# A mixture-of-experts stage in a vision tower: the routing weights come to all partitions by a broadcast transfer instead of a selecting matmul

## The reference, cut to what matters

```python
topk_idx, topk_w = _gate(x, gate_w, gate_bias)      # 8 of 32 experts for each token, with weights
g = jnp.einsum('th,eih->eti', x, expert_gate)
u = jnp.einsum('th,eih->eti', x, expert_up)
outs = jnp.einsum('eti,ehi->eth', jax.nn.silu(g) * u, expert_down)
outs_t = jnp.transpose(outs, (1, 0, 2))
gathered = jnp.take_along_axis(outs_t, topk_idx[:, :, None], axis=1)
final = (gathered * topk_w[:, :, None]).sum(1)
shared = _mlp(residuals, shared_gate, shared_up, shared_down)
return final.reshape(orig_shape) + shared
```

## Time and profile before

| | |
|---|---|
| median of 3 runs | 427.67 us (426.64 to 428.51) |
| profiled execution, span from first to last instruction | 425.9 us |
| TensorE busy | 394.3 us, 93% |
| VectorE busy | 265.4 us, 62% |
| ScalarE busy | 187.7 us, 44% |
| GpSimd busy | 145.9 us, 34% |
| mean granted TensorE clock | 0.988 of full speed |

### The profile page before, as it was taken

How to read it: one execution, slowest core, us unless ns; L and a number is a source line. 1 busy time by engine, 2 the same in 40 slices (tenths; PEclk the granted TensorE clock), 3 DMA queues, 4 the chain that set the end, 5 groups by cost and what they waited for, 6 DMA issues and landing times.

```text
span 425.9 us, 8795 instructions
## 1 busy us (share of the span) xinstructions
PE 394.3 (93%) x3362; PEld 319.3 (75%) x3362; DVE 265.4 (62%) x529; ACT 187.7 (44%) x401; POOL 145.9 (34%) x119
## 2 busy tenths in 40 slices
PE   8998699898999799999999999999988999999684
PEld 6654478656786689999999999999986765567342
DVE  0368886688876875555555555555554648854776
ACT  0244832248242534444444444444435378734161
POOL 0145300363032153333333333333384246720102
PEclk9999999998999999999999999999999999999799
DMA  8930000200051022222222222232000000000001
GB/s 303 339 148 0 3 3 2 98 1 3 4 186 37 2 74 75 75 75 74 74 74 74 74 74 74 74 79 68 0 0 2 0 2 2 2 2 2 0 0 58
DMA packets 9547, 23.79 MB, mean 56 GB/s; under 512 B 1264, under 2 KB 3248, under 8 KB 9008
## 3 DMA queue, kind: packets, MB, share of 16 engines
q1 hardware_dynamic: 7632, 21.49, 15.8%
q10 hardware_dynamic: 1888, 1.93, 1.3%
HBM read 22.81 MB, written 0.61 MB: 55 GB/s over the span
## 4 chain that ended last, share of the span: by engine, by line
PE 71%; DVE 21%; issue 4%; ACT 4%; POOL 0%; DVEq 0%; ACTq 0%
PE psum L1073 70%; DVE xn L764 3%; DVE rc L838 3%; DVE nt L761 2%; DVE rn L817 1%; DVE nt L759 1%; DVE rn L816 1%; ACT region L716 1%; DVE region L839 1%; DVE xc L750 1%; DVE ra L807 1%; DVE km L1055 1%; ACT sq L532 1%; PE psum L1225 1%; DVE km L827 1%
## 5 line engine op out<-in xcount | busy, mean ns | idle before, releaser
L1073 PE MATMUL psum<-xh,split_all 128*128 128x296 f32 x544 | 122.1, 299 | 1.4 <-DVE rt L918 1.3
L431 POOL TENSOR_TENSOR split_all<-km,split_all 128x768 fp32r<-128x768 f32 x34 | 62.7, 1845 | 119.8 <-ACT split_all L645 119.8
L1073 PEld LDWEIGHTS psum<-xh,split_all 128*128 128x128 f32 x544 | 91.4, 188 | 1.9 <-DVE rt L918 1.9
L1073 PE MATMUL psum<-xl,split_all 128*128 128x296 f32 (+1 forms) x288 | 84.8, 299 | 0.0
L1073 PE MATMUL psum<-ah,split_all 128*128 128x296 f32 x272 | 73.5, 324 | 2.9 <-DVE al L981 2.4
L665 ACT ACTIVATE ah<-rt 128x296 fp32r<-128x296 f32 x68 | 30.7, 452 | 94.7 <-DVE rt L979 88.0
L1073 PEld LDWEIGHTS psum<-xl,split_all 128*128 128x128 f32 (+1 forms) x288 | 53.2, 187 | 3.2 <-issue 3.2
L976 DVE TENSOR_TENSOR rb<-ra,psum 128x296 f32<-128x296 f32 x64 | 29.6, 462 | 41.3 <-PE psum L1073 29.9
L981 DVE TENSOR_TENSOR al<-rt,ah 128x296 fp32r<-128x296 f32 x64 | 31.6, 495 | 33.2 <-ACT ah L665 33.2
L1073 PEld LDWEIGHTS psum<-ah,split_all 128*128 128x128 f32 x272 | 48.6, 192 | 4.1 <-DVE al L981 2.8
L1073 PE MATMUL psum<-al,split_all 128*128 128x296 f32 x136 | 40.6, 299 | 0.0
(11 more groups left out here) (181 smaller groups left out, 612.5 us busy)
## 6 DMA issues: line engine op xcount, KB each, us to landing
km<-in_experts SPq DMA_DIRECT2D x34, 384.0 KB, 3.0
w_sb<-in_w SPq DMA_DIRECT2D x2, 1024.0 KB, 11.8
region<-in_x SPq DMA_DIRECT2D x6, 296.0 KB, 5.5
region<-in_g_wo SPq DMA_DIRECT2D x1, 1024.0 KB, 4.8
region<-in_l_wo SPq DMA_DIRECT2D x1, 1024.0 KB, 4.8
region<-in_w_lin ACTq DMA_DIRECT2D x6, 128.0 KB, 6.7
qkv_sb<-in_qkv_w SPq DMA_DIRECT2D x1, 768.0 KB, 6.0
cst<-in_consts ACTq DMA_DIRECT2D x1, 504.5 KB, 6.8
```

What stands on the lines that cost most here:

```text
L431: nc.gpsimd.tensor_tensor(wl[i], ring[i], wh[i].bitcast(f32), ALU.subtract)\
L1073: return nc.tensor.matmul(out_, lhsT, rhs, start=start, stop=stop, skip_group_check=True)
```

## The change

The weights are no longer split into three bf16 parts. They are transposed in f32 by products with the identity, copied to `wrow` (now 32 rows x 640 columns, f32, in two copies), written to a DRAM tensor `weights`, and read back for each expert by one transfer that puts its row of 592 values on all 128 partitions of a slot of `wb`, a ring of four. VectorE's second product reads `wb` in place of the PSUM bank. For the first two experts (units 2 and 3) the weights still come by a selecting product, now in f32 and into banks 6 and 7. `up_sums` loses the selecting matmul. All broadcasts are issued by SP, between the loads of the experts' weights.

```diff
+        wrow = sb("wrow", [EXPERTS, TT * P])
+        wb = sb("wb", [P, NRING, T])
...
-            with sp.Fori(1, UNITS // NRING) as r:
+            def load_expert(u, expert):
+                i = u % NRING
+                sp.wait_ge(s_wsh, u + 1 - NRING)
+                sp.wait_ge(s_wsl, u + 1 - NRING)
+                sp.dma_start(ring[i], expert).then_inc(s_ring[i], 16)
+
+            def spread_weights(i, row):
+                sp.dma_start(wb[:, i, :], row.broadcast_to([P, T])).then_inc(s_wb[i], 16)
+
+            for u in range(NRING, 2 * NRING):
+                if u == NRING + 2:
+                    sp.wait_ge(s_wrow, 2)
+                    sp.dma_start(weights, wrow[:, 0:T]).then_inc(s_wout, 16)
+                    sp.wait_ge(s_wout, 16)
+                    for i in range(NRING):
+                        spread_weights(i, weights[NRING + i - SHARED:NRING + i - SHARED + 1, :])
+                load_expert(u, experts[u, :, :])
+            with sp.Fori(2, UNITS // NRING) as r:
...
+                    sp.wait_ge(s_act, r * (2 * NRING) + 2 * (i + 1 - NRING))
+                    spread_weights(i, weights[bass.ds(r * NRING + (i - SHARED), 1), :])
...
-            link(nc.vector.tensor_tensor(wts[:], wts[:], bc(wsum[:].unsqueeze(2), [P, TT, EXPERTS]), ALU.mult))
-
+            nc.vector.tensor_tensor(wts[:], wts[:], bc(wsum[:].unsqueeze(2), [P, TT, EXPERTS]), ALU.mult)\
+                .then_inc(s_wts, 1)
             shared_product(2, 0)
-            link(nc.vector.tensor_copy(wparts[:, :, 0:EXPERTS], wts[:]))
-            link(nc.vector.tensor_tensor(wres[:], wts[:], wparts[:, :, 0:EXPERTS], ALU.subtract))
-            link(nc.vector.tensor_copy(wparts[:, :, EXPERTS:2 * EXPERTS], wres[:]))
-            link(nc.vector.tensor_tensor(wres[:], wres[:], wparts[:, :, EXPERTS:2 * EXPERTS], ALU.subtract))
-            nc.vector.tensor_copy(wparts[:, :, 2 * EXPERTS:3 * EXPERTS], wres[:]).then_inc(s_wp, 1)
             shared_product(3, 1)
             dve.wait_ge(s_wt, 1)
-            nc.vector.tensor_copy(wrow[0:96, :], ps[7][:].bitcast(bf16)[0:96, 0:TT * P]).then_inc(s_wrow, 1)
+            nc.vector.tensor_copy(wrow[:, 0:(TT - 1) * P], ps[7][0:EXPERTS, :]).then_inc(s_wrow, 1)
+            nc.vector.tensor_copy(wrow[:, (TT - 1) * P:TT * P], ps[6][0:EXPERTS, 0:P]).then_inc(s_wrow, 1)
...
-            def expert_unit(n, j):
+            def expert_unit(n, j, weight):
 
                 dve.wait_ge(s_sg, n + 1)
                 dve.wait_ge(s_u, n + 1)
                 ins = nc.vector.tensor_tensor(gu[:, j, :], sg[:, j, :], ps[5][:, 0:HALF], ALU.mult)
                 ins.then_inc(s_mulc, 1)
                 dve.wait_ge(s_mulc, n + (1 - 2 * SHARED))
-                nc.vector.tensor_tensor(act[:, j, :], gu[:, j, :], ps[6][:, 0:HALF], ALU.mult).then_inc(s_act, 1)
+                nc.vector.tensor_tensor(act[:, j, :], gu[:, j, :], weight, ALU.mult).then_inc(s_act, 1)
                 dve.wait_ge(s_ah, n + 1)
                 nc.vector.tensor_tensor(al[:, j, :], act[:, j, :], ah[:, j, :].bitcast(f32), ALU.subtract)\
                     .then_inc(s_al, 1)
 
-            with dve.Fori(1, UNITS // 2) as r:
-                for j in range(4):
-                    expert_unit(r * 4 + j, j % 2)
+            for u in range(SHARED, NRING):
+                for j in range(2):
+                    dve.wait_ge(s_sel, 2 * (u - SHARED) + j + 1)
+                    expert_unit(2 * u + j, j, ps[6 + j][:, 0:HALF])
+            with dve.Fori(1, UNITS // NRING) as r:
+                for i in range(NRING):
+                    dve.wait_ge(s_wb[i], r * 16)
+                    for j in range(2):
+                        expert_unit(r * (2 * NRING) + (2 * i + j), j, wb[:, i, half(j)])
+            for u in range(UNITS - UNITS % NRING, UNITS):
+                dve.wait_ge(s_wb[u % NRING], u // NRING * 16)
+                for j in range(2):
+                    expert_unit(2 * u + j, j, wb[:, u % NRING, half(j)])
...
-                if wait_for_weights:
-                    pe.wait_ge(s_wrow, 1)
-                if not shared:
-                    sel = select_bf[0:96, bass.ds(u, 1)].broadcast_to([96, P])
-                    ins = mm(ps[6][:, 0:HALF], sel, wrow[0:96, half(hf)], True, True)
                 ins.then_inc(s_u, 1)
+
+            def selected_weights(u, hf):
+
+                n = 2 * u + hf
+                pe.wait_ge(s_wrow, 2)
+                if u > SHARED:
+                    pe.wait_ge(s_act, n - 1)
+                sel = const("ident", EXPERTS)[:, u - SHARED:u - SHARED + 1].broadcast_to([EXPERTS, P])
+                mm(ps[6 + hf][:, 0:HALF], sel, wrow[:, half(hf)], True, True).then_inc(s_sel, 1)
...
-            pe.wait_ge(s_wp, 1)
+            pe.wait_ge(s_wts, 1)
             for t in range(TT):
-                ins = nc.tensor.transpose(ps[7][:].bitcast(bf16)[0:96, t * P:(t + 1) * P], wparts[:, t, :],
-                                          ident_bf)
+                ins = mm((ps[7][0:EXPERTS, t * P:(t + 1) * P] if t < TT - 1 else ps[6][0:EXPERTS, 0:P]),
+                         wts[:, t, :], const("ident"), True, True)
             ins.then_inc(s_wt, 1)
-            up_sums(2, 2, 0, wait_for_weights=True)
+            up_sums(2, 2, 0)
             down_sums(1, 1, 1, shared=True)
+            selected_weights(2, 0)
             for u in (2, 3):
                 up_sums(u, u, 1)
+                selected_weights(u, 1)
                 down_sums(u, u, 0)
                 up_sums(u + 1, (u + 1) % NRING, 0)
+                if u + 1 < NRING:
+                    selected_weights(u + 1, 0)
                 down_sums(u, u, 1)
```

More of the change, by code:

```diff
@@ L67 @@
     ("b1", FC), ("b2", C), ("gate_bias", EXPERTS)])
-NBF = P + S + UNITS
+NBF = P + S
+SELECTED = 2
 def program(nc, x, w_lin, consts, consts_bf, vecs, g_wq, g_down, g_k, g_v, g_wo, l_wq, l_wk, l_wv, l_wo,
-            gate_w, experts, qkv_w, out_w, w1, w2, out):
+            gate_w, experts, qkv_w, out_w, w1, w2, weights, out):
     f32, f32r, bf16 = mybir.dt.float32, mybir.dt.float32r, mybir.dt.bfloat16
@@ L164, in program @@
         wsum = sb("wsum", [P, TT])
-        wparts = sb("wparts", [P, TT, 3 * EXPERTS], bf16)
-        wrow = sb("wrow", [P, TT * P], bf16)
+        zeros = sb("zeros", [P, HALF], bf16)
+        wrow = sb("wrow", [EXPERTS, TT * P])
         xh = sb("xh", [P, C, T], f32r)
@@ L268, in program @@
         s_sig = sem("router_scores_ready")
-        s_wp = sem("weight_parts_ready")
-        s_wt = sem("weight_parts_transposed")
+        s_wts = sem("weights_ready")
+        s_wt = sem("weights_transposed")
         s_wrow = sem("weight_rows_ready")
+        s_wout = sem("weight_rows_stored")
+        s_sel = sem("weights_selected")
+        s_wb = [sem(f"weights_on_all_partitions{i}") for i in range(NRING)]
         s_xh = sem("token_high_parts_ready")
@@ L276, in program @@
         s_g = sem("gate_summed")
-        s_u = sem("up_and_weight_summed")
+        s_u = sem("up_summed")
         s_sg = sem("silu_ready")
@@ L365, in _ @@
                         .then_inc(s_ring[i], 16)
+                    sp.wait_ge(s_act, r * (2 * NRING) + 2 * (i + 1 - NRING))
+                    spread_weights(i, weights[bass.ds(r * NRING + (i - SHARED), 1), :])
             for u in range(UNITS - UNITS % NRING, UNITS):
[L367 to L370, removed]
+                load_expert(u, experts[u, :, :])
+                sp.wait_ge(s_act, 2 * (u + 1 - NRING))
+                spread_weights(u % NRING, weights[u - SHARED:u - SHARED + 1, :])
             for hf in range(2):
@@ L855, in normalise_outputs @@
                                         bc(den.unsqueeze(3), [P, HALFPOS, 2, HD]), ALU.mult).then_inc(s_on, 1)
-            nc.vector.memset(wparts[:], 0.0).then_inc(s_zero, 1)
+            nc.vector.memset(zeros[:], 0.0).then_inc(s_zero, 1)
             dve.wait_ge(s_cst, 48)
@@ L1290, in _ @@
             pe.wait_ge(s_zero, 1)
-            zeros = wparts[:].rearrange("p t n -> p (t n)")
             keep_busy(7, START_BUSY, zeros[:, 0:P], zeros[:, 0:HALF])
@@ L1356, in three, with up_sums @@
                 return mm(out_, w_lo, x_hi, False, stop)
-            def up_sums(u, i, hf, first=False, shared=False, wait_for_weights=False):
+            def up_sums(u, i, hf, first=False):
                 n = 2 * u + hf
@@ L1397, in _ @@
             pe.wait_ge(s_xs, 1)
-            up_sums(0, 0, 0, first=True, shared=True)
+            up_sums(0, 0, 0, first=True)
             seed(1)
@@ L1532, in constants @@
     b[:, P:P + S] = np.where(real[:, None] & (token[:, None] > np.arange(S)[None, :]), -32768.0, 0.0)
-    for u in range(SHARED, UNITS):
-        for part in range(3):
-            b[part * EXPERTS + u - SHARED, P + S + u] = 1.0
     return c, b
@@ L1624 @@
     out = nc.dram_tensor("out", (P, C, T), mybir.dt.float32, kind="ExternalOutput").ap()
-    program(nc, *args, out)
+    weights = nc.dram_tensor("weights", (EXPERTS, T), mybir.dt.float32, kind="Internal").ap()
```

(1 more changed line is left out.)

8 lines of the change are left out of this document (3 added, 5 removed).

## The result

| | before | after |
|---|---|---|
| median of 4 runs | 428.0 us (426.64 to 428.51) | 448.7 us (448.33 to 449.46) |
| span of the profiled execution | 425.9 us | 447.0 us |
| ratio after to before, 95% interval | | 1.0494 (1.0469 to 1.0519) |

What follows compares the result with a forecast made beforehand. The prediction took TensorE's matmul slots as the bound, and after the change the chain through the held product. Terms 3.4+14.0+2.5 = +19.9 on the 425.9 us span gave 445.8, as median 447.5 us; range 437 to 453.

Steps and rivals of the forecast that it cites:

- head: Units 2 and 3 and the transposes, now in f32, before unit 4: +3.4 us, bounds +2 to +5.
- middle: 27 steps from unit 4 to 31: product held by GpSimd's subtraction, unit 5.68 us instead of 5.16, +14.0 us.
- tail: Units 31 to 33: GpSimd's back-to-back instructions reading SBUF hold VectorE's products and low parts: +2.5 us, bounds 0 and +4.
- A+3.43: End of the second half's held product, instead of A+2.57; A is ScalarE's L665 start for a unit's first half.
- Rival (a): Second product under GpSimd's subtraction: the hold does not set the unit time, matmul slots do; 424 us, chance 0.08.
- Rival (c): Same product: slower unit shifts the subtraction, held only half of 0.86 us, unit 5.25; 436 us, chance 0.10.
- the f32 selection: Four selecting products of units 2 and 3, each two instructions, 0.58 us instead of 0.137: +1.8 us.
- The transposes: Five transposes in the head become ten f32 instructions, 1.3 us against 0.44: +0.9 us, bounds +0.5 to +2.5.
- the stall at the first selection: In the head, the next half's up sums find the product late: some 0.7 us stall of TensorE.
- The transfers: Stores, broadcasts and loads on SP: hidden, nothing taken; DMA share rises from 0.26 to 0.47, over a longer unit less.
- Rival (b): Transfers late at the start: unit 4 or the split of expert 6 waits some 5 us; 452 us, chance 0.09.
- Rival (d): TensorE's clock falls since it idles 14% of the stage: 6 us more, 453 us, chance 0.05.

Runs made afterwards that it cites:

- Experiment 1: Kernel before, with only the second product's second input moved from PSUM to a tile of ones in SBUF, selecting matmuls kept, no broadcasts: 449.92 us, ratio 1.0528.
- experiment 2: Changed kernel, with the second product of units 4 to 33 reading PSUM banks instead of wb, all broadcasts still issued: 424.19 us, ratio 0.9914 to before.
- experiment 3: Changed kernel, with GpSimd's subtraction of units 4 to 33 replaced by three memsets that read nothing: 426.18 us, ratio 0.9946 to before.
- Experiment 4: Changed kernel, with GpSimd's subtraction in four instructions of 192 columns instead of one of 768: 437.27 us, ratio 1.0235 to before.
- experiment 7: Changed kernel, with the four selecting products of units 2 and 3 in bf16 instead of f32: 446.33 us, ratio 1.0416 to before.
- experiment 9: Changed kernel, with weights' low parts on VectorE, three-part bf16 selection for units 2 and 3, GpSimd's quantisation in 16 pieces, two expert loads ahead of broadcasts: 420.53 us.
- experiment 10: Kernel before, with the weights' low parts on VectorE and the quantisation in 16 pieces, selecting matmuls and PSUM factor kept: 426.66 us, ratio 0.9976.
- experiment 6: Kernel before, with only the low parts of the weights of units 4 to 33 moved from GpSimd to VectorE: 429.01 us, ratio 1.0029.
- experiment 8: Changed kernel, with GpSimd's subtraction of units 4 to 33 made to wait for a second half's product: 460.27 us, ratio 1.0765 to before.

## Why the prediction was right

Point by point, by the steps of the prediction, in us of the profiled executions:

| step | forecast | measured |
|---|---|---|
| head, A4 | +3.4 (2 to 5) | 173.75 - 169.25 = +4.5; from A0 26.21 - 22.09 = +4.1 |
| middle, 27 units | +14.0 (5.68 a unit) | 153.79 - 139.50 = +14.3 (5.696) |
| tail from A31 | +2.5 (0 to 4) | 18.60 - 16.02 = +2.6 |
| sum | +19.9 | +21.4, span +21.1 |

*The unit.* The mechanism and its price were read from two rows elsewhere in the trace and held: the product ends at A+3.46 (forecast A+3.43), the unit takes 5.696 us. Experiment 1 gives the whole loss from the operand's place alone, experiments 2 and 3 take the loss away by removing one side of the collision each. Rival (a) is refuted as a forecast and confirmed as what lies beneath: experiment 2 gives 424.19 where it said 424. Rival (c), a half hold, does not occur in this order of work. Experiment 4 makes one, but only in every second unit, and that it lands at 437, near the 436 of (c), is in part luck: its units cost 3.4 us more than those of before, where (c) had 2.4, and its head 4.4 to A4, where (c) had 3.4.

*The head.* The sign was right, the size too small. Of the 4.5 us, 0.4 lie ahead of the stage (A0 is at 147.16 before and at 147.54 after) and say nothing of the change; of the 4.1 that are left the forecast had 3.4. The term that was mis-sized is the f32 selection, taken as 2 x 0.29 us. The timeline of TensorE in after:

```profile
155.93 1.28 PE L1100 MATMUL psum<-cst,wts 128*32 128x128 f32 x10
...
162.38 0.30 PE L1100 MATMUL psum<-xh,split_all 128*128 128x296 f32 x1
162.61 0.76 PE L1100 MATMUL psum<-wrow,cst 32*128 32x296 f32 x2
163.30 0.41 PE L1100 MATMUL psum<-ah,split_all 128*128 128x296 f32 x1
163.54 0.30 PE L1100 MATMUL psum<-al,split_all 128*128 128x296 f32 x1
```

From 162.38 to 163.54 are 1.16 us, two slots (0.27) and the selection: 0.89. Four of them, at 0.89 - 0.137, are +3.0 instead of +1.8. By experiment 7 only 1.8 of the 3.0 are f32; the rest comes with the 32 rows (last section). The transposes, from the last matmul before them to the second one behind them, take 1.67 instead of 0.60 us, +1.1 (forecast +0.9), the stall at the first selection 0.3 (forecast 0.7), in sum 4.4. The first half of unit 4 has one selection less in front of it (-0.14), and the down sums ahead of the transposes start 7.39 us behind A0 instead of 7.49: 4.1, all of it. Here two errors of the forecast, the selection too cheap by 1.2 and the stall too dear by 0.4, partly cancelled.

*The tail.* The order worked out came true. From A31 (327.54) the low part ends at A+5.6, the product at 7.8, the low part at 9.9, the product at 11.9 (forecast 5.5, 7.7, 9.8, 11.9), each 0.3 us after the end of the GpSimd instruction that lies over it (two L479, two L482, ending at A+5.3, 7.5, 9.5 and 11.6):

```profile
327.54 0.45 ACT L686 ACTIVATE ah<-rt 128x296 fp32r<-128x296 f32 x1 [1.45 <-DVE rt L996]
...
330.65 4.36 POOL L479 TENSOR_SCALAR w_sb<-w_sb,inv 128x2048 f32<-128x2048 f32 x2
...
331.51 1.64 DVE L998 TENSOR_TENSOR al<-rt,ah 128x296 fp32r<-128x296 f32 x1 [0.52 <-ACT ah L686]
...
333.56 1.76 DVE L996 TENSOR_TENSOR rt<-rb,wb 128x296 f32<-128x296 f32 x1
...
334.98 2.10 POOL L482 TENSOR_SCALAR w1q<-w_sb 128x2048 bf16<-128x2048 f32 x1
...
335.84 1.55 DVE L998 TENSOR_TENSOR al<-rt,ah 128x296 fp32r<-128x296 f32 x1 [0.52 <-ACT ah L686]
...
337.80 1.67 DVE L996 TENSOR_TENSOR rt<-rb,wb 128x296 f32<-128x296 f32 x1
...
346.14 0.30 PE L1100 MATMUL psum<-ah,split_all 128*128 128x296 f32 x1
```

*The transfers.* Rival (b) did not come: the four first broadcasts and the loads behind them had landed by about 170, the first product to need one starts at 173.25. The share of the DMA engines is 0.41 in the stage (forecast 0.47 or less). A load's landing grew from 3.0 to 4.1 us, not forecast, and hidden. The prediction mixed two units here: a broadcast is 296 KB as the profile counts, not 303, and the share by its sum 0.46, which changes nothing.

*The clock.* Rival (d) did not come: TensorE idles 6.5% of the stretch by its busy time (3.39 of 52 us; the slots alone would fill 4.9 of 5.7, since recorded matmuls overlap), and the granted clock stays at 1.00.

## What to carry to other kernels

Before moving an operand of a VectorE instruction from PSUM to SBUF, look in the timeline for a GpSimd instruction with SBUF inputs that lies above its start, and look for any instruction of the same trace with two SBUF inputs in that place: its stretched duration is what the chain behind it has to bear (here 0.85 us, of which 0.52 a unit showed against the kernel before, since the old chain, with the product ending at A+2.57, had 0.34 us of slack). The slots of the selecting matmuls, 8.2 us by the prediction, can be won, and 6.1 us of them stayed after their own costs (experiments 9 and 10), but only together with the change that takes the GpSimd reads out of the loop; ask of each such move which other two-input instruction it lands on (experiments 6 and 8). A mean or a median of a group hides such a hold; the minimum and maximum of the group show it at once.

## What was not expected of the hardware

A product of 32 rows, or to 32 output partitions, costs more among full ones than a full one does. In experiment 9 a bf16 product of 96 rows to 128 output partitions adds 0.14 us to its neighbours, and one of 96 rows to 32 output partitions, of the same 296 columns, adds 0.43, with 0.23 us from the start before it, 0.23 to the start behind it and 0.24 to the one after:

```profile
158.30 0.30 PE L1130 MATMUL psum<-qcopy,cstb 96*128 96x296 bf16 x1
158.34 0.39 PE L1130 MATMUL psum<-ah,split_all 128*128 128x296 f32 x1
158.57 0.30 PE L1130 MATMUL psum<-al,split_all 128*128 128x296 f32 x1
...
159.12 0.30 PE L1130 MATMUL psum<-ah,split_all 128*128 128x296 f32 x1
159.35 0.30 PE L1130 MATMUL psum<-qcopy,cstb 96*32 96x296 bf16 x1
159.58 0.40 PE L1130 MATMUL psum<-xh,split_all 128*128 128x296 f32 x1
159.82 0.30 PE L1130 MATMUL psum<-xl,split_all 128*128 128x296 f32 x1
```

In experiment 7 the bf16 selection of 32 rows to 128 output partitions costs the same 0.43 (159.02 to 159.72, less 0.27). So of the 0.75 us by which a selection became dearer about 0.3 are its 32 rows and 0.46 are f32; four times 0.46 is the 1.8 us of experiment 7. The Trainium skill, "TensorEngine Tiling (Array Packing)", section "Key Properties", states that changing the tiling mode drains TensorE; that a product of 32 rows or to 32 output partitions is such a change would fit these gaps, but no run here tries it by itself, so the cause is not shown.
